# Moving split operands from SBUF partitions to SBUF partitions, and a group statistic from TensorE to GpSimd

## What is computed

```python
# layer 0
y  = conv1d_over_channels(mean(x, (2, 3)), w_c)          # 5 taps
yc = sigmoid(x * y[:, :, None, None])
sa = sigmoid(conv2d([mean_c(yc), max_c(yc)], w_s))       # 5x5
x  = yc * sa + x
# layer 1: GroupNorm, 32 groups of 2 channels, then attention
mean, var = group statistics of x;  xn = (x - mean) * rsqrt(var + 1e-5) * gn_w + gn_b
q, k, v = split(qkv_w @ xn + qkv_b)                      # 4 heads of 16
attn = softmax(q^T k / 4);  out = proj_w @ (v attn^T) + proj_b
return x + out
```

## Time and profile before

| | us |
|---|---|
| median of 3 runs | 187.82 (187.49 to 189.54) |
| profiled execution, as timed on the device | 188.28 |
| its span, first to last instruction | 186.5 |
| TensorE matmul busy | 167.9 (90%) |
| VectorE busy | 141.5 (76%) |
| ScalarE busy | 120.4 (65%) |
| GpSimd busy | 112.3 (60%) |

### The profile page before, as it was taken

How to read it: one execution, slowest core, us unless ns; L and a number is a source line. 1 busy time by engine, 2 the same in 40 slices (tenths; PEclk the granted TensorE clock), 3 DMA queues, 4 the chain that set the end, 5 groups by cost and what they waited for, 6 DMA issues and landing times.

```text
span 186.5 us, 4811 instructions
## 1 busy us (share of the span) xinstructions
PE 167.9 (90%) x1518; PEld 105.6 (57%) x1518; DVE 141.5 (76%) x295; ACT 120.4 (65%) x250; POOL 112.3 (60%) x214
## 2 busy tenths in 40 slices
PE   7788985998786999999999999999999999998791
PEld 2255765464463577675766767676675655553230
DVE  0838669378866298998989899898997979777433
ACT  3072641452376387978988798898877967648730
POOL 5992184679685537888788788878876270101110
PEclk9969999999999699999999999999999999999967
DMA  3941403668279655556364564646554563310001
GB/s 76 357 136 40 114 7 101 184 202 221 86 226 223 184 116 162 156 184 172 119 199 129 193 177 156 191 124 192 159 174 133 178 207 102 99 33 29 23 11 56
DMA packets 20070, 26.25 MB, mean 141 GB/s; under 512 B 4268, under 2 KB 16980, under 8 KB 20052
## 3 DMA queue, kind: packets, MB, share of 16 engines
q1 hardware_dynamic: 19472, 25.47, 47.0%
q10 hardware_dynamic: 580, 0.55, 1.1%
HBM read 17.35 MB, written 8.42 MB: 138 GB/s over the span
## 4 chain that ended last, share of the span: by engine, by line
PE 67%; DMA 10%; DVE 6%; POOL 6%; issue 4%; ACT 3%; SPq 2%; POOLq 0%; ACTq 0%
PE bank L710 16%; PE bank L684 14%; PE bank L696 13%; PE bank L720 7%; PE bank L739 5%; DMA qs<-maxrow 4%; PE bank L730 3%; PE bank L623 2%; DMA parts_dram<-parts 2%; DMA con<-consts 2%; DMA ks<-parts_dram 2%; DVE maps L477 1%; PE bank L752 1%; POOL tapprod L308 1%; ACT pt L424 1%
## 5 line engine op out<-in xcount | busy, mean ns | idle before, releaser
L560 DVE TENSOR_REDUCE negmax<-bank 128x2 bf16<-128x512 f32 x128 | 83.5, 679 | 18.9 <-PE bank L684 17.4
L424 ACT ACTIVATE pt<-bank 128x512 f32<-128x512 f32 x128 | 72.8, 595 | 24.7 <-PE bank L696 24.7
L696 PE MATMUL bank<-qs,ks 97*128 97x256 bf16 x256 | 49.4, 275 | 5.3 <-DMA qs<-maxrow 3.3
L684 PE MATMUL bank<-ks,qs 96*128 96x256 bf16 x256 | 49.8, 276 | 1.9 <-DMA ks<-parts_dram 1.2
L710 PE MATMUL bank<-pt,vs 128*32 128x256 f32 x512 | 35.7, 399 | 0.0
L684 PEld LDWEIGHTS bank<-ks,qs 96*128 96x128 bf16 x256 | 21.7, 100 | 24.3 <-DVE negmax L560 15.5
L696 PEld LDWEIGHTS bank<-qs,ks 97*128 97x128 bf16 x256 | 23.7, 98 | 13.5 <-ACT pt L424 5.6
L321 POOL TENSOR_TENSOR xall<-yo,xall 128x256 f32 (+1 forms) x15 | 10.9, 725 | 31.2 <-ACT yo L444 31.2
L348 POOL TENSOR_TENSOR rest<-z,parts 128x512 f32<-128x512 f32 x15 | 17.3, 1155 | 11.1 <-issue 8.1
L710 PEld LDWEIGHTS bank<-pt,vs 128*32 128x32 f32 x512 | 15.2, 112 | 12.8 <-ACT pt L424 3.1
L600 PE MATMUL bank<-warm 128*128 128x512 bf16 x60 | 20.1, 452 | 1.4 <-POOL warm L298 1.4
(11 more groups left out here) (70 smaller groups left out, 215.6 us busy)
## 6 DMA issues: line engine op xcount, KB each, us to landing
parts_dram<-parts SPq DMA_DIRECT2D x48, 128.0 KB, 2.1
ks<-parts_dram SPq DMA_DIRECT2D x16, 192.0 KB, 3.0
qs<-parts_dram SPq DMA_DIRECT2D x16, 192.0 KB, 3.2
xall<-x SPq DMA_DIRECT2D x4, 512.0 KB, 5.9
qs<-parts_dram SPq DMA_DIRECT2D x16, 128.0 KB, 2.7
ks<-parts_dram SPq DMA_DIRECT2D x16, 128.0 KB, 2.7
out<-xall SPq DMA_DIRECT2D x16, 128.0 KB, 2.1
gate<-gate_dram SPq DMA_DIRECT2D x6, 256.0 KB, 3.9
```

The source lines that it names most:

```text
L424: nc.scalar.activation(pt[:, (u + LEAD) % UNITS, :, :].rearrange("p t n -> p (t n)"), st_bank[u % 2][:, :], ACT.Exp, scale=SCALE).then_inc ...
L560: nc.vector.tensor_reduce(negmax[:, slot(1), column:column + TILES], s_bank[u % 2][:, :].rearrange("p (t n) -> p t n", t=TILES), AX.X, ALU ...
L684: mm = pe.matmul(s_bank[u % 2][:, t * N:(t + 1) * N], qs[0:KQ, slot(1), h, a, t * P:(t + 1) * P], ks[0:KQ, slot(1), h, a, :], start=True, ...
L696: mm = pe.matmul(st_bank[u % 2][:, t * N:(t + 1) * N], ks[0:KQ + 1, slot(d), h, a, t * P:(t + 1) * P], qs[0:KQ + 1, slot(d), h, a, :], sta ...
```

## The change

The DRAM tensor and its writes go. Each of the six blocks of `qs` and of `ks` is filled by a DMA of its own, directly from 64 partitions of `parts` (1 KB each) into 16 partitions of the tile (four pieces of 1 KB each): twelve DMAs of 64 KB a pair in place of three of 128 KB and six of 64, 128 or 192 KB. SP's order in a turn becomes: maxrow; the four copies of part 1 and the two of part 2 for pair k+2; the store; in turns 0 and 1 the two gate reads; the six copies of part 0 for pair k+3. The last wait until part 1 of that pair is made, which stands behind GpSimd's wait for `st_ready`, since that wait protects the slot of the ring; that wait moves up, ahead of scale and shift. ScalarE's wait for the old write goes. The second small matmul goes; GpSimd makes the half difference with one more addition ahead of the square.

```diff
+TERMS = ((0, 0), (1, 0), (2, 0), (0, 1), (1, 1), (0, 2))
-            aside = {(0, 2): lambda: gate_read(sp, 2), (1, 2): lambda: gate_read(sp, 3)}
+            aside = {(0, 1): lambda: gate_read(sp, 2), (1, 1): lambda: gate_read(sp, 3)}
             def turn(k, slot, has, lap):
+                def stack(d, part):
+                    r = slot(d)
+                    for row, terms in enumerate(TERMS):
+                        for tile, g in ((qs, 0), (ks, 1)):
+                            if terms[g] == part:
+                                sp.dma_start(tile[row * HD:(row + 1) * HD, r, :, :, :].rearrange("p h a n -> p h (a n)"),
+                                             parts[C * g:C * (g + 1), r, part, :]).then_inc(stack_in[r], 16)
-                if has(2):
-                    wait(sp, parts_out[0], 16 * (k + 3))
-                    stack(ks, 1, 0, 3, part=0)
-                    stack(qs, 0, 5, 1)
                 if has(0):
                     wait(sp, mrow_ready, k + 1)
                     sp.dma_start(qs[KQ:KQ + 1, slot(0), :, :, :]..., maxrow[:, slot(0), :]).then_inc(mrow_in, 16)
                 if has(2):
-                    wait(sp, parts_out[1], 16 * (k + 3))
-                    stack(qs, 0, 3, 2)
-                    stack(ks, 1, 3, 2, part=1)
-                    wait(sp, parts_out[2], 16 * (k + 3))
-                    stack(qs, 0, 0, 3)
-                    stack(ks, 1, 5, 1, part=2)
-                if has(3):
-                    wait(sp, p1_ready, k + 4)
-                    part_write(0)
+                    wait(sp, split_step, 3 * (k + 2) + 2)
+                    stack(2, 1)
+                    wait(sp, split_step, 3 * (k + 3))
+                    stack(2, 2)
                 if has(-3):
...
+                stands_in(aside, k, 1)
                 if has(3):
-                    wait(sp, split_step, 3 * (k + 3) + 2)
-                    part_write(1)
-                    wait(sp, split_step, 3 * (k + 4))
-                    part_write(2)
-                stands_in(aside, k, 2)
+                    if isinstance(k, int) and k < 1:
+                        sp.wait_ge(p1_ready, k + 4)
+                    else:
+                        wait(sp, split_step, 3 * (k + 3) + 2)
+                    stack(3, 0)
# GpSimd
-                    nc.gpsimd.tensor_tensor(sq[:, :], gmv[:, 2:3], gmv[:, 2:3], ALU.mult).then_inc(sq_ready, 1)
+                    nc.gpsimd.tensor_tensor(gmd[:, :], mv[:, 0:1], gmv[:, 0:1], ALU.add).then_inc(gmd_ready, 1)
                     nc.gpsimd.tensor_tensor(posvar[:, :], eps[:, :], gmv[:, 1:2], ALU.subtract).then_inc(posvar_ready, 1)
+                    wait(pool, gmd_ready, k + 5)
+                    nc.gpsimd.tensor_tensor(sq[:, :], gmd[:, :], gmd[:, :], ALU.mult).then_inc(sq_ready, 1)
...
+                if on_pool:
+                    wait(pool, st_ready, UNITS * k)
                 if has(4):
                     wait(pool, rstd_ready, k + 5)
...
-                    wait(pool, st_ready, UNITS * k)
# ScalarE, u = 0
-                        wait(act, parts_out[0], 16 * k)
# VectorE, u = 4
-                        wait(dve, gs_ready, k + 5)
+                        wait(dve, gmd_ready, k + 5)
# TensorE
-                        wait(pe, stack_in[slot(1)], lap(1) * 96)
+                        wait(pe, stack_in[slot(1)], lap(1) * 2 * SLOTS * 16)
-                    pe.matmul(gs_psum[:, 0:2], groupavg, mv[:, :], start=True, stop=True)
-                    mm = pe.matmul(gs_psum[:, 2:3], groupsplit, mv[:, 0:1], start=True, stop=True)
+                    mm = pe.matmul(gs_psum, groupavg, mv[:, :], start=True, stop=True)
```

More of the change, by code:

```diff
@@ L47 @@
 C_GROUP = C_MEAN + 2
-C_SPLIT = C_GROUP + P
-C_END = C_SPLIT + P
+C_END = C_GROUP + P
 TSTRIDE = KPAD + P
@@ L62, in program @@
         bank = [ctx.enter_context(nc.psum_tensor(f"bank{i}", [P, 512], F32)) for i in range(8)]
-        parts_dram = nc.dram_tensor("parts_dram", [RING, 3, 2, HD, HEADS * 2 * N], BF16).ap()
         gate_dram = nc.dram_tensor("gate_dram", [IMAGES, N], F32).ap()
@@ L75, in program @@
         groupavg = con[:, C_GROUP:C_GROUP + P]
-        groupsplit = con[:, C_SPLIT:C_SPLIT + P]
         identb = sb("identb", [P, P], BF16)
@@ L94, in program @@
         mv = sb("mv", [P, 2])
-        gmv = sb("gmv", [P, 3])
+        gmv = sb("gmv", [P, 2])
+        gmd = sb("gmd", [P, 1])
         sq = sb("sq", [P, 1])
@@ L133, in program @@
         y_psum = bank[7][:, 0:256]
-        gs_psum = bank[6][:, 400:403]
+        gs_psum = bank[6][:, 400:402]
         rows_in, con_in, ident_in, wall_in, vec_in, sel_in = sem("rows_in"), sem("con_in"), sem("ident_in"), sem("wall_in"), sem("vec_in"), sem("sel_in")
@@ L157, in program @@
         split_step = sem("split_step")
-        parts_out, stack_in = [sem(f"parts_out{i}") for i in range(3)], [sem(f"stack_in{r}") for r in range(RING)]
+        stack_in = [sem(f"stack_in{r}") for r in range(RING)]
         s_ready, max_done = sem("s_ready"), sem("max_done")
@@ L163, in program @@
         norm_step, y_ready = sem("norm_step"), sem("y_ready")
-        sq_ready, posvar_ready, vareps_ready, rstd_ready, gn_scale, gn_mean = sem("sq_ready"), sem("posvar_ready"), sem("vareps_ready"), sem("rstd_ready"), sem("gn_scale"), sem("gn_mean")
+        gmd_ready, sq_ready, posvar_ready, vareps_ready, rstd_ready, gn_scale, gn_mean = sem("gmd_ready"), sem("sq_ready"), sem("posvar_ready"), sem("vareps_ready"), sem("rstd_ready"), sem("gn_scale"), sem("gn_mean")
         yo_ready, out_ready = sem("yo_ready"), sem("out_ready")
@@ L801, in constants @@
     c[:, C_GROUP:C_GROUP + P] = 0.5 * (i // 2 == j // 2)
-    c[:, C_SPLIT:C_SPLIT + P] = 0.5 * (i // 2 == j // 2) * np.where(i == j, 1, -1)
     c[:, C_MEAN:C_MEAN + 2] = (i // C == np.arange(2)[None, :]) / C
```

## The result

The changed kernel takes 208.35 us in the median of four executions (206.69 to 209.44), against 188.68 for the one before beside it: 1.106 times as long, with a 95% interval of 1.094 to 1.118 (the ratio leaves out one slow execution of the kernel before, of 192.12 us; that of the medians is 1.104). It is slower, as forecast, but by 20 us where 5.4 were forecast, and outside the range.

What follows compares the result with a forecast made beforehand. SP's issue queue was to bound full turns at 8.81 us against TensorE's 7.96: +6.8 by turn 13's maxrow, less 1.4 given back, +5.4 on 187.8, so 193.2 us; range 183 to 199 for 8 in 10.

Steps and rivals of the forecast that it cites:

- What bounds it: In every full turn, SP's queue of twelve copy issues was to become the bound in place of TensorE's 7.96 us.
- The price of an issue: Each new copy on SP's queue was taken at 0.62 us for issue and gap, bounds 0.38 and 0.66.
- Rival B: SP's copies inside SBUF cost only 0.34 + 0.04 us, so SP binds nothing; 182 to 183.5 us; chance 0.24.
- Sum 8.81 ... SP becomes the bound: SP's full turn: twelve copies 7.44, maxrow 0.58, store and its gaps, together 8.81 us against TensorE's 7.96.
- the predicted 161.45: Forecast issue time of turn 13's maxrow, against 154.69 before: +6.8 us, counted from turn 0's maxrow at 46.65.
- the 0.60 that I struck out: Turn 0's `s(0)` waits 0.60 us for a stack; without DRAM's leg that stall was to go.
- a sign of being right: At the start, first maxrow issues no later than today (46.65, 56.0), with the drift beginning behind turn 3.
- rival D: TensorE's idling before each `s(0)` lowers the clock in every turn: 7.7 us on top, 201 us; chance 0.08.
- Gives back 1.4 once: The next turn's `s(0)` can start 2.1 to 2.7 us before maxrow, against today's 0.98, giving back 1.4 once.
- GpSimd and the moved wait: GpSimd's chain grows 0.33 us to 7.78, hidden under SP's turn; the moved `st_ready` wait costs nothing or a few tenths.
- The matmul: One small matmul fewer saves TensorE 0.18 us a turn: nothing under SP's bound, otherwise 2.0 us in all.
- Bytes: Operands move 12.6 MB in place of 18.9; DMA share falls from 47% to about 35%, no bound before or after.

Runs made afterwards that it cites:

- the statistics part alone: Against the kernel before, only the second small matmul removed and one GpSimd addition added: 186.94 us, ratio 1.006.
- the run of shapes: The kernel before plus four DMAs each of eleven shapes behind its last store, each awaited; issues took 0.30 to 0.33 us SBUF-DRAM, 0.46 to 0.62 inside SBUF.

## Why the prediction was right and wrong

**What bounds it: right.** SP had little to spare, twelve issues overran it, TensorE waits for copies before `s(0)`, the share of DMA falls to 0.30, and half the bytes leave the turn at 8.98. Half the copies bring the time back, and four idle copies a turn take it away from the kernel before.

**The price of an issue: nearly right, for a wrong reason.** 0.62 was taken, 0.636 measured; undisturbed turns are 8.97 in place of 8.81. By the prediction's own count of 156 issues this is 2.5 us. But the reason given, that a side of 16 or 64 partitions makes it dear, fell with the run of shapes: 16 partitions from DRAM cost 0.30. Rival B was weighed by the same wrong mark; it fails because no copy inside SBUF is as cheap as 0.38 with its gap.

**"Sum 8.81 ... SP becomes the bound": the step that failed is that the turn was taken as constant.** The sum multiplied one turn by ten and put what disturbs single turns at nothing: the prolonged issues, TensorE's wait for a stack at the start, and the low clock behind a late maxrow. Against the predicted 161.45 the maxrow of turn 13 was issued at 174.40, 12.95 us later; turns 3 to 12 took 9.38 us in the mean.

*Prolonged issues.* In each kernel some issues last 1.0 to 1.9 us in place of 0.6. In the kernel before and in the changed one, beside each other:

```profile
100.14 1.46 SPq L250 DMA_DIRECT2D ks<-parts_dram  x1
```

```profile
112.10 1.60 SPq L247 DMA_DIRECT2D qs<-parts  x1
```

Both are of turn 6. The kernel before has them in turns 0, 2, 3, 4, 6, 11 and 13, the changed one in 0, 1, 4, 6, 11 and 13, its repeat in 0, 2, 3, 4, 6, 11 and 13. The kernel before with the statistics part alone has them in 0, 2, 5 and 6. So they do not come with the copies, and the turns are alike but not the same. In the DMA view of 111.8 to 114 of the changed kernel stands

```profile
q1 hardware_dynamic: 158, 0.13, 18.9%
q8 instruction: 1, 0.02, 4.0%
```

one packet of an instruction queue. The view from 119.28 to 155.37, the second lap of the loop (turns 7 to 10), has none, and no prolonged issue either:

```profile
q1 hardware_dynamic: 4507, 3.66, 30.1%
```

The twelve traces of this case, all but that of the shapes, settle how far this goes. After the first 40 us SP has 72 issues of 0.9 us and more in them, and every one overlaps in time a packet of an instruction queue; of the 2152 issues under 0.65 us 154 do. In the second lap of the loop no issue lasts over 0.83 us in any of them, and the only packets of those queues begin in its last 0.1 us. So prolonged issues go with these packets, and a second lap of the same instructions has neither. That the packets bring code, and that this is what holds the issue up, is inferred: no run has moved or removed one. Before, SP's 1.6 us of slack swallowed most of it. With SP as the bound each is lost in full: 5.2 us of the 12.95, in turns 0 to 12.

*The start.* Maxrow of turn 0 was forecast at 46.65 and came at 48.34, 1.7 late: TensorE's wait for a stack didn't go but grew to 1.55 us, since the last copy for pair 1 took 5.62 us to land. This is the 0.60 that I struck out. The copies there run beside gate reads, and the run with the gates on ScalarE's queue shows how those fill the DMA engines. Maxrow of turn 1 came at 58.46, for the 56.0 or earlier that was named as a sign of being right. Then maxrow of turn 2, behind twelve copies, two gate reads and a prolonged issue of 1.94 us, was issued at 70.22:

```profile
72.29 0.59 PE L684 MATMUL bank<-qs,ks 97*128 97x256 bf16 x2 [3.00 <-DMA qs<-maxrow]
```

In that wait of 3.00 us, at 71.1, the clock fell, and TensorE ran at 1.2 GHz to 81, the 0.51 of the first view. SP had to wait until 80.63 for turn 3's maxima, 2.2 us. This is rival D, not in each turn but once at this length; I had given it 8%. In the loop TensorE's waits of some 0.4 us leave the clock at 1.00. Behind one of 1.41 us in turn 11, at 162.68, it was half for 3.4 us; behind one of 1.42 at 116.22 it stayed.

*Sum of the 12.95:* pace 2.5, prolonged issues 5.2, start 1.7 and 2.2, and 1.35 left. Of the size of this rest are single holes in SP's queue: 0.45 us between the two gate reads of turn 1, and 0.42, 0.21 and 0.37 ahead of the next maxrow in turns 6, 10 and 12, where 0.04 is usual. The maxima had been copied earlier each time, so SP didn't wait for them, and what fills the holes is not shown.

**"Gives back 1.4 once": wrong.** The lead is there: `s(0)` at 134.66, maxrow at 137.25, 2.59 us in place of 0.98. But it is worth nothing, since TensorE stops again at u = 4 for the maxrow itself (the row at 139.25 waits 0.35 for it). The last maxrow issues sit on the path to the end: from turn 13's on, 32.4 us remain, against 31.8 before. Together with the 0.6 this is 2.0 us. 5.4 + 12.95 + 2.0 = 20.35 accounts for the span's 20.3.

**GpSimd and the moved wait: right that they cost nothing,** and the chain is not even 0.33 longer, as z32 was the later input. **The matmul: right that it is worth nothing under SP's bound;** the 2.0 us it should bring otherwise were 0.05 us a turn, 0.6 us in all, within the scatter.

**Bytes: right in the main.** 31.2% share, for about 35% forecast at an equal rate, over the span for 19.1 MB, as against 47.0% for 25.5.

## What to carry to other kernels

Count an issuing queue like an engine: issues times their measured duration against the turn, before a transfer is split into more of them; bytes and share of the DMA engines say nothing on it. A queue that is filled close to its turn also loses its cushion, so every disturbance it used to absorb turns into time: the kernel before had some 1.6 us to spare in 8 and hid its disturbances, and with two more copies it didn't. Keep such a rest, or move a few issues to a queue whose engine computes beside them. A round trip that no recurring wait shows is hidden, and shortening it brought nothing here.

## What the runs showed of the hardware that I had not expected

- Issued alone, a copy inside SBUF holds SP's queue 0.46 to 0.62 us, a plain transfer between SBUF and DRAM 0.30 to 0.33, with 16 or 128 partitions and with 64 to 512 KB alike. Right behind a copy the same store took 0.58 in place of 0.34.
- A DMA issued by ScalarE (0.57 us) overlapped ScalarE's own computing: activations at 117.92 and 118.39 beside issues at 117.81 and 118.41.
- All 72 issues of 0.9 us and more, in twelve traces, overlap a packet of an instruction queue, and in the loop's second lap there are neither.
- With waits of TensorE of 2.3 and 3.0 us the clock fell to half; with one or two of 0.4 us in every turn it stayed at 1.00. Waits of 1.4 us went either way.
